# Two stacked cross-attention layers on one core: layer 1 follows layer 0 at 116 steps instead of 124, and its ring loads are held closer to their use

## The reference

```
# layer 0
q, k_t, v_t = x @ W_q, ctx[:-4] @ W_k, ctx[:-4] @ W_v
probs_t = softmax(q k_t^T / 4)
qsem = l2norm(probs_t @ ctx[:-4])              # 512 wide, per head and query
fused = q k_ip^T / 4 + 0.5 * qsem @ l2norm(ctx[-4:])^T
out = probs_t @ v_t + (softmax(fused) * mask) @ v_ip
x1 = out @ W_out + b_out + x
# layer 1, queries from x1
out = softmax(q k^T / 4) @ v  +  softmax(q k_ip^T / 4) @ v_ip     # 77 text keys, 947 ip keys
result = out @ Wo^T + bo + x1
```

## Time and profile before

| what | value |
|---|---|
| median of three executions | 3422.0 us |
| the profiled execution, own time | 3425.3 us |
| its span, first to last instruction | 3423.5 us |
| PE busy | 3334.1 us, 97% |
| DVE busy | 1989.3 us, 58% |
| ACT busy | 1836.1 us, 54% |
| POOL busy | 1091.0 us, 32% |
| DMA queues' traffic | 271.3 MB, mean 79 GB/s |

### The profile page before, as it was taken

One profiled execution on the slowest core, in us unless ns is written; L12 is line 12 of the kernel. 1 busy time (PEld: TensorE's weight loads), 2 busy tenths in 40 slices (PEclk: granted clock), 3 DMA queues, 4 the chain that ended last, 5 costly groups with the idle time before them and its releaser, 6 DMA issues.

```text
span 3423.5 us, 65769 instructions
## 1 busy us (share of the span) xinstructions
PE 3334.1 (97%) x24736; PEld 2897.2 (85%) x24736; DVE 1989.3 (58%) x5509; ACT 1836.1 (54%) x4014; POOL 1091.0 (32%) x933
## 2 busy tenths in 40 slices
PE   6999999999999999999999999999999999999978
PEld 4888988887888888888888888888888898989855
DVE  4444455556556566565656556655565656555577
ACT  2333333555555555555655556555555556565668
POOL 3111001334332333333333232333423322322368
PEclk8999999999999999999999999999999999999999
DMA  6433923233358322233358422323328532222242
GB/s 190 118 76 70 95 54 101 72 96 88 80 72 104 78 69 71 72 98 82 89 69 76 94 73 71 81 76 100 88 66 77 67 59 51 60 47 53 46 86 53
DMA packets 648783, 271.30 MB, mean 79 GB/s; under 512 B 479666, under 2 KB 599426, under 8 KB 648468
## 3 DMA queue, kind: packets, MB, share of 16 engines
q1 hardware_dynamic: 646356, 267.06, 38.9%
q10 hardware_dynamic: 2112, 0.03, 0.0%
HBM read 187.97 MB, written 79.04 MB: 78 GB/s over the span
## 4 chain that ended last, share of the span: by engine, by line
PE 89%; DVE 5%; ACT 2%; POOL 1%; issue 1%; DMA 1%; SPq 0%; POOLq 0%; ACTq 0%; DVEq 0%
PE acc L1180 9%; PE acc L1173 9%; PE acc L1176 8%; PE acc L1175 8%; PE acc L1181 8%; PE acc L1174 7%; PE score L1140 4%; PE score L1224 4%; PE spare L1224 4%; PE score L1142 4%; PE av L1211 3%; PE av L1215 3%; PE spare L1265 2%; PE spare L1314 2%; PE score L1265 2%; PE score L1314 2%
## 5 line engine op out<-in xcount | busy, mean ns | idle before, releaser
L1398 ACT ACTIVATE prob<-score 128x512 f32<-128x512 f32 x1219 | 728.9, 598 | 1187.5 <-PE score L1142 1182.7
L1839 POOL TENSOR_TENSOR prob_lo<-prob,prob_hi 128x512 fp32r<-128x512 f32 x624 | 811.9, 1305 | 1473.7 <-ACT prob_hi L1401 1472.9
L1173 PE MATMUL acc<-tok_v,prob_hi 128*128 128x300 f32 x2240 | 908.2, 405 | 2.1 <-ACT prob_hi L1401 2.1
L1175 PE MATMUL acc<-tok_lo,prob_hi 128*128 128x256 f32 (+1 forms) x2560 | 759.8, 297 | 0.0
L1180 PE MATMUL acc<-tok_v,prob_lo 128*128 128x278 f32 (+1 forms) x2560 | 745.4, 291 | 0.0
L1401 ACT ACTIVATE prob_hi<-score 128x512 fp32r<-128x512 f32 x1219 | 726.0, 596 | 0.0
L1176 PE MATMUL acc<-tok_lo,prob_hi 128*128 128x256 f32 (+1 forms) x2560 | 719.0, 281 | 0.0
L1181 PE MATMUL acc<-tok_v,prob_lo 128*128 128x256 f32 (+1 forms) x2560 | 717.8, 280 | 0.0
L1174 PE MATMUL acc<-tok_v,prob_hi 128*128 128x256 f32 x2240 | 627.6, 280 | 0.0
L1176 PEld LDWEIGHTS acc<-tok_lo,prob_hi 128*128 128x128 f32 (+1 forms) x2560 | 483.6, 189 | 8.6 <-issue 2.3
L1175 PEld LDWEIGHTS acc<-tok_lo,prob_hi 128*128 128x128 f32 (+1 forms) x2560 | 484.4, 189 | 5.4 <-issue 3.0
(11 more groups left out here) (336 smaller groups left out, 4979.4 us busy)
## 6 DMA issues: line engine op xcount, KB each, us to landing
k_ring<-k_scr SPq DMA_DIRECT2D x160, 384.0 KB
tok_v<-v_scr SPq DMA_DIRECT2D x158, 176.0 KB, 3.4
v_ring<-v_scr SPq DMA_DIRECT2D x160, 148.5 KB, 3.4
ctx_t<-in_ctxT SPq DMA_DIRECT2D x16, 1024.0 KB, 9.0
q_ring<-q_scr SPq DMA_DIRECT2D x160, 96.0 KB
v_scr<-v_stage SPq DMA_DIRECT2D x28, 440.0 KB, 2.5
v_scr<-v_stage SPq DMA_DIRECT2D x36, 330.0 KB, 10.1
tok_stage<-in_ctx SPq DMA_DIRECT2D x28, 256.0 KB, 3.1
```

The costliest lines, as they stand in the source:

```text
L1173: e.matmul(out_a[:, 0:SEG + VCOLS], p_hi, tok_v[0:kk, c, seg, v_lo:v_lo + SEG + VCOLS], start=first, stop=False)
L1175: e.matmul(out_a[:, t0:t0 + SEG], p_hi, tok_lo[0:kk, c, seg * SEG:(seg + 1) * SEG], start=False, stop=False)
L1398: e.activation(prob[:, es, :], bank_s[:, :], ACT.Exp, scale=SCALE)
L1839: e.tensor_tensor(prob_lo[:, ps, :], prob[:, es, :], prob_hi.bitcast(F32)[:, ps, :], ALU.subtract).then_inc(s_low[1], 1)
```

## The change

Two numbers. `LAG_UNITS` is 116, and the bound on ring loads now holds for every part of layer 1: 13 steps ahead of the part's first step for part 8, 12 for part 15, 18 for the others.

```diff
-LAG_UNITS = 124
+LAG_UNITS = 116
...
+LOAD_AHEAD = {B: 13, LAST: 12}
...
-            load_at.setdefault(max(at, start_of[place[(u, 0)]] - (12 if u == LAST else 14)) if u in (B, LAST) else at, []).append(g)
+            load_at.setdefault(max(at, start_of[place[(u, 0)]] - LOAD_AHEAD.get(u, 18)) if u >= B else at, []).append(g)
```

## The result

The changed kernel took 3444.3 us (median of 4, 3442.1 to 3446.1), the kernel before on the same chip 3423.1 us. The ratio is 1.0059, with a 95% interval of 1.0046 to 1.0071: **slower by 0.6%, some 21 us**, where +1 us was forecast and 3432 us was the upper end of the range. The profiled execution took 3442.9 us, its span is 3441.0 us. Between the two profiled spans lie 17.5 us, and these are what can be traced.

A forecast was written before the change was run, and what follows sets the result against it. PE was taken to bound the lead and the woven stretch, with no engine full in most of the tail. Terms +8.0 - 11.5 + 0 + 3.5 + 1.0 = +1.0 us gave 3423 us, range 3412 to 3432.

The forecast's parts named there:

- +8.0 us for eight woven steps: Woven stretch, where PE is the limit: eight added layer-1 steps cost 1.00 us each, +8.0 us.
- -11.5 us for the tail: Tail, first q piece to part 15: eight steps fewer, each saving part 15's pace of 1.44 us, -11.5 us.
- the full average pace of the bound: Tail: upper bound of 1.89 us a step, 15.1 us for eight; as faster rival 3415 us, chance 0.2.
- the forecast's 31 to 32: Tail: a sign, 31 to 32 us between the first q piece and part 15 instead of 43.
- 0 for the ring loads of part 15: Start of part 15: ring load just hidden behind PE's 15 to 16 us of work, 0, up to 4 us if not.
- the rival of the q chain: Before part 15: PE waits at the first maxima product for its ring load; 3429 us, up to 3434.5; chance 0.2.
- +3.5 us at x and q of parts 9 and 14: Woven stretch: PE waits 1.6 to 1.8 us for `x_in_lo` before q, twice, +3.5 us, bounds 0 and 6.
- +1 us for loads 18 steps ahead: Parts 9 to 14, first group: loads 18 steps ahead instead of 28 cost between 0 and 6 us, taken as +1.
- the squeezed maxima: First group of parts 9 to 14: 8 maxima products in 5 steps instead of 10 or 11, a burst on DVE.
- an average cover of 46 us: Woven stretch: 18 steps of 2.55 us give 46 us, against at most 7.0 us that a load needs.
- "Nothing of layer 0 is added ... nothing for these": Lead: the same 8 layer-0 steps now have a layer-1 step between them; no cost for the layer-0 steps.
- a woven stretch that grew by more than 16 us: Woven stretch: a sign that the price of a woven step or of its waits is off; under 6 us likewise.

The follow-up runs named there:

- run 12: As run 10, with the bulk loads of text and weights issued behind a part's residual loads; 3429.0 us, ratio 1.0010 to the kernel before.
- run 3: The changed kernel (distance 116) with the ring-load bound at 14 steps instead of 18; 3446.3 us, ratio 1.0058 to the kernel before.
- run 8: As run 6, with maxima from 2 steps behind their load instead of 4; 3436.1 us, ratio 1.0034 to the kernel before.
- run 1: The kernel before (distance 124) with only the new bound, 18 steps for parts 9 to 14; 3433.8 us, ratio 1.0028.
- run 9: The changed kernel with value blocks at least 4 steps apart; 3436.1 us, ratio 1.0035 to the kernel before.
- run 5: The kernel before (distance 124) with projections of parts 9 to 14 due one window earlier; 3434.8 us, ratio 1.0027.
- run 6: The changed kernel with the ring-load bound at 17 steps instead of 18; 3435.6 us, ratio 1.0032 to the kernel before.
- run 10: The changed kernel with the bound at 17 and value blocks at least 4 steps apart; 3432.6 us, ratio 1.0025 to the kernel before.
- run 13: The same three edits as run 12 (bound 17, spaced blocks, residuals first) at distance 124; 3443.1 us, ratio 1.0049 to the kernel before.
- run 2: The changed kernel (distance 116) with the bound lifted for parts 9 to 14; 3465.3 us, ratio 1.0117 to the kernel before.

## Why the prediction was wrong

- **+8.0 us for eight woven steps**: right. Up to the end of part 1 the changed kernel has 7.7 us more of PE busy time, and the kernels at 116 are 8.5 to 10.8 us longer with the waits.
- **-11.5 us for the tail**: the mechanism was right, the size too small. Measured -15.4, the full average pace of the bound 15.1; the other kernels at 116 gave from -11.4 (run 12) to -15.3 (run 3). What the clock does in the tail differs between them. The first q piece is at 3296.6, 38.5 us behind layer 0 (41.7 before), and from there to part 15 it takes 31 us, the forecast's 31 to 32: 3.2 of the further 3.9 us lie ahead of q, where the forecast had nothing. The granted clock of that stretch was 0.96, where it was 0.84 before; that this made the 3.2 us is not shown.
- **0 for the ring loads of part 15**: right; PE had no wait for them, and the rival of the q chain fell with it.
- **+3.5 us at x and q of parts 9 and 14**: right to the tenth, 3.5 us in 2. That the sum fits so closely is luck, for the pieces are 0.9 and 2.6 us and not 1.7 each. And the second of these waits was followed by a fall of the clock, 1.7 us more.
- **+1 us for loads 18 steps ahead**: the failed step, in two ways. It priced only the squeezed maxima, for which run 8 shows no price, and it dismissed a late load with an average cover of 46 us, where the first product stands 13 us behind the load; run 1 has the edit, with the later due times that come with it, at +10 us.
- **"Nothing of layer 0 is added ... nothing for these"**: the second failed step. The layer-0 steps are the same, but the background work between them was moved: value blocks from 10 us to 6 or 7 us apart on two slots, x and q into a pressed window. The order lists would have shown it; the prediction read them only at x and q. Measured are some 8 us for the blocks (run 9) and 9 to 10 for the window (runs 5 and 6, partly the same microseconds: both together, run 10, are 12).

Against the changed kernel's +21: woven steps +9 to +11, tail -15, loads later (run 1) +10; the crowded window and blocks 12 (run 10), and residual loads behind bulk loads 4 (run 12, which a fall of the clock may blur). These add up to 20 to 22. That it closes so well is no proof: the edits need not be additive, and run 1's +10 holds waits for residual loads itself. What is open: how the +10 us of run 1 divide between the late load and the later due times, why the middle is still 6.4 us longer with no direct DMA wait left (run 13), 4.4 us of longer busy time outside the clock's falls, and why the start of layer 1 waits for `row_parts` at 124 with a bound of 13 and at 132.

Of the signs named, "a woven stretch that grew by more than 16 us" is the one that came: 33.5 us.

## What to carry to other kernels

In a kernel whose order comes from a planner, a change of one distance moves every job that is due by it. Compare the spacing of each background job's pieces with the time that its buffers take to come free (here two slots, each taken for 13.7 us, 9.6 of it the landing, want 6.8 us a piece, and the pieces stood 6.2 apart), not only the pieces near the edit. Where TensorE is at 99%, average cover says little: ask at each place what stands one instruction behind the thing that may be late, and price a wait of 2 us as up to 3.7, since the clock may fall behind it.

## What was unexpected of the hardware

- PE is busy 98 to 99% from 430 us to the end of layer 0, and yet single short waits of it were followed by a fall of the clock to 1.2 GHz. In the changed kernel and runs 1, 9 and 12, waits of 1.97 to 2.55 us were followed by 3.4 us at 1.2 GHz, so by another 1.7 us of loss, in 8 of 12 cases. Over all 16 traces it was 22 of the 36 waits of 1.9 to 2.6 us, and each of the 11 longer ones (2.9 to 6.2 us). The reverse isn't strict: three falls (548 us in runs 2 and 10, 1303 us in run 5) had no wait of even 1.85 us ahead of them. What sets the other 14 apart stayed open.
- Two kinds of stores of value blocks, and a load, by their landing (KB each, then us):

```profile
v_ring<-v_scr SPq DMA_DIRECT2D x160, 148.5 KB, 3.4
...
v_scr<-v_stage SPq DMA_DIRECT2D x28, 440.0 KB, 2.7
v_scr<-v_stage SPq DMA_DIRECT2D x36, 330.0 KB, 10.0
```

The smaller store lands after 10.0 us, the larger one after 2.7: the size alone doesn't tell how long a slot is taken. Their shapes differ. The larger one is a block of layer 0 and writes 128 whole rows of 3520 bytes; the smaller one is a block of layer 1 and writes 33 of every 44 columns, 2560 pieces of 132 bytes. It is so in the woven stretch alone too (2.1 to 4.1 us for 24 stores, 7.8 to 15.7 for 27). No run changes the shape alone, so that the small pieces are the reason isn't shown, but a layout in whole rows would be the next thing to try.

- Issuing the bulk loads 2 steps later on the same queue took away a wait of 7.6 us for the small loads that had stood around and behind them (run 12 against run 10).
